# A start-up reordering in a joint-softmax classifier kernel: two products move to GpSimd, two sums are split, idle matmuls are cut, first products and tail waits are reordered

## The reference

```
variables = [softmax(p) for p in split(logits, 4)]      # v0, v1, v2, v3: 512 x 16 each
flat = outer(v0, v1, v2, v3).reshape(512, 65536)
num_y_joint = einsum('bj,by->yj', flat, y_true)          # 100 x 65536
num_joint = sum(flat, axis=0)                            # 65536
prob_y_joint = clip(max(num_y_joint, 1e-6) / max(num_joint, 1e-6), 0, 1)
probs = einsum('yj,bj->by', prob_y_joint, flat)          # 512 x 100
```

## Time and profile before

| | |
|---|---|
| time, median of 3 runs | 534.98 us (534.86 to 535.18) |
| time of the profiled execution | 535.27 us |
| its span in the profile | 533.2 us |
| PE busy | 529.1 us, 99% |
| DVE busy | 296.3 us, 56% |
| ACT busy | 41.7 us, 8% |
| POOL busy | 23.1 us, 4% |

### The profile page before, as it was taken

The page is one execution under the profiler, slowest core; times in us unless marked ns, Lnnn a source line. Parts: engine busy times, 40 slices in busy tenths (PEclk is TensorE's granted clock), DMA queues, the critical chain, the costliest instruction groups (busy, mean ns, idle before and its releaser), DMA issues.

```text
span 533.2 us, 8646 instructions
## 1 busy us (share of the span) xinstructions
PE 529.1 (99%) x3115; PEld 305.0 (57%) x3115; DVE 296.3 (56%) x763; ACT 41.7 (8%) x96; POOL 23.1 (4%) x21
## 2 busy tenths in 40 slices
PE   9999999999999999999999999999999999999997
PEld 5555555555555555555555555555555555555555
DVE  7986766764585444444467544444446544444446
ACT  7950000000200000000020000000001000000000
POOL 0000000000140000000032000000004000000000
PEclk9999999999999999999999999999999999999999
DMA  2944434220000000000000000000000000000000
GB/s 45 159 80 79 59 62 79 46 54 1 1 0 1 1 0 0 0 0 0 1 0 1 1 0 0 0 0 0 0 0 1 1 0 0 0 0 0 1 1 17
DMA packets 34771, 9.21 MB, mean 17 GB/s; under 512 B 34496, under 2 KB 34752, under 8 KB 34752
## 3 DMA queue, kind: packets, MB, share of 16 engines
q1 hardware_dynamic: 34752, 8.93, 9.5%
HBM read 0.34 MB, written 0.20 MB: 1 GB/s over the span
## 4 chain that ended last, share of the span: by engine, by line
PE 99%; DVE 0%; issue 0%; POOL 0%; DVEq 0%; POOLq 0%
PE joined L454 16%; PE joined L456 16%; PE joined L455 16%; PE numbers L446 16%; PE numbers L447 16%; PE numbers L448 16%; PE numbers L470 1%; PE numbers L476 1%; PE numbers L479 1%; PE numbers L473 1%; DVE acc L413 0%; PE numbers L576 0%; PE numbers L573 0%; PE numbers L572 0%; PE joined L567 0%; PE joined L564 0%
## 5 line engine op out<-in xcount | busy, mean ns | idle before, releaser
L456 PE MATMUL joined<-r_hi,pt_lo 128*128 128x400 f16 x504 | 167.6, 332 | 0.0
L455 PE MATMUL joined<-r_lo,pt_hi 128*128 128x400 f16 x504 | 167.6, 332 | 0.0
L454 PE MATMUL joined<-r_hi,pt_hi 128*128 128x400 f16 x504 | 167.5, 332 | 0.0
L446 PE MATMUL numbers<-q_hi,p_hi 128*128 128x404 f16 x492 | 164.8, 335 | 0.0
L448 PE MATMUL numbers<-q_hi,p_lo 128*128 128x404 f16 x492 | 164.0, 333 | 0.0
L447 PE MATMUL numbers<-q_lo,p_hi 128*128 128x404 f16 x492 | 163.9, 333 | 0.0
L333 DVE TENSOR_SCALAR den<-numbers 128x4 f32<-128x4 f32 x128 | 20.7, 162 | 211.4 <-PE numbers L448 211.3
L345 DVE SCALAR_TENSOR_TENSOR r_lo<-ratio,r_hi 128x400 f16<-128x400 f32 x128 | 78.3, 612 | 4.4
L338 DVE SCALAR_TENSOR_TENSOR ratio<-numbers,inv 128x400 f32<-128x400 f32 x128 | 73.5, 574 | 4.4
L455 PEld LDWEIGHTS joined<-r_lo,pt_hi 128*128 (+1 forms) x504 | 49.2, 98 | 36.3
L454 PEld LDWEIGHTS joined<-r_hi,pt_hi 128*128 (+1 forms) x504 | 49.1, 97 | 36.3
(11 more groups left out here) (53 smaller groups left out, 87.1 us busy)
## 6 DMA issues: line engine op xcount, KB each, us to landing
pt_hi<-p_hi SPq DMA_TRANSPOSE x16, 3.1
pt_lo<-p_lo SPq DMA_TRANSPOSE x16, 3.2
labels<-in_r_y_true_dram SPq DMA_DIRECT2D x1, 200.0 KB, 3.0
out_dram<-acc SPq DMA_DIRECT2D x1, 150.0 KB, 1.8
x<-in_r_logits_dram SPq DMA_DIRECT2D x1, 128.0 KB, 2.1
out_dram<-acc SPq DMA_DIRECT2D x1, 50.0 KB, 1.5
```

The lines of the kernel that those rows point to most:

```text
L446: pe.matmul(out, p_at(p_hi, tile, k), q_at(q_hi, g, k), start=(k == 0), stop=False)
L454: pe.matmul(out, p_at(pt_hi, tile, k), r_hi[:, slot, :], start=first, stop=False)
L455: pe.matmul(out, p_at(pt_hi, tile, k), r_lo[:, slot, :], start=False, stop=False)
L456: last = pe.matmul(out, p_at(pt_lo, tile, k), r_hi[:, slot, :], start=False, stop=final)
```

## The change

GpSimd no longer zeroes `idle` (VectorE does) and, behind the wait for the first exponentials, makes p23 of chunks 0 and 1 in two instructions with a semaphore of their own (`p23_first`). VectorE drops `make_p23(0, 2)` and sums v2, v3 and then v0, v1 in two reductions. ScalarE waits for `p23_first`. TensorE has 24 idle matmuls (14, 5, 3, 2) in place of 31, and the second batch waits for the exponentials and not for p23. Some of the first 48 products change place, none is added or dropped. In the tail the waits for `added` and for `half_ready` change order in the source.

```diff
-        IDLE_START, IDLE_EXPS, IDLE_V0, IDLE_Q = 18, 6, 4, 3
+        IDLE_START, IDLE_EXPS, IDLE_V0, IDLE_Q = 14, 5, 3, 2
...
-            pool.memset(idle[:, :], 0.0).then_inc(idle_set, 1)
             pool.memset(labels[:, :, CLASSES:CW], 1.0).then_inc(ones_set, 1)
             pool.memset(acc[:, :, :], 0.0).then_inc(acc_set, 1)
+            pool.wait_ge(exps, 1)
+            for k in range(2):
+                pool.tensor_tensor(p23[:, k, :].rearrange("p (c d) -> p c d", d=S),
+                                   ek[:, k, 2, :].unsqueeze(2).broadcast_to([LANES, S, S]),
+                                   ek[:, k, 3, :].unsqueeze(1).broadcast_to([LANES, S, S]),
+                                   ALU.mult).then_inc(p23_first, 1)
...
-            act.wait_ge(p23_made, 1)
+            act.wait_ge(p23_first, 1)
             first_p_hi(0, 0)
+            act.wait_ge(p23_first, 2)
             first_p_hi(0, 1)
...
+            dve.memset(idle[:, :], 0.0).then_inc(idle_set, 1)
             dve.wait_ge(logits_in, 16)
...
             dve.wait_ge(exps, 1)
-            make_p23(0, 2)
+            dve.tensor_reduce(sums[:, :, 2:4], ek[:, :, 2:4, :], AX.X, ALU.add).then_inc(reduced, 1)
             dve.wait_ge(exps, 2)
-            dve.tensor_reduce(stat[:, 1, :], x[:, :, :], AX.X, ALU.add).then_inc(reduced, 1)
-            dve.wait_ge(reduced, 1)
+            dve.tensor_reduce(sums[:, :, 0:2], ek[:, :, 0:2, :], AX.X, ALU.add).then_inc(reduced, 1)
+            dve.wait_ge(reduced, 2)
             dve.tensor_reduce(whole[:, :], sums, AX.X, ALU.mult).then_inc(reduced, 1)
...
             for a in range(AG):
+                dve.wait_ge(added, KC * AG + a)
                 if a % HA == 0:
                     dve.wait_ge(half_ready, a // HA + 1)
-                dve.wait_ge(added, KC * AG + a)
                 add(KC - 1, a, numbers[a // HA], a % HA)
...
             pe.wait_ge(idle_set, 1)
             idle_turns(IDLE_START)
-            pe.wait_ge(p23_made, 1)
+            pe.wait_ge(exps, 1)
             idle_turns(IDLE_EXPS)
```

More of the change, by code:

```diff
@@ L115, in joint_classifier @@
         v0n_made = sem("v0n_made")
+        p23_first = sem("p23_first")
         p23_made = sem("p23_made")
@@ L247, in _ @@
             first_p_hi(1, 1)
-            act.wait_ge(p23_made, 2)
+            act.wait_ge(p23_made, 1)
             first_p_hi(0, 2)
@@ L348, in _ @@
             dve.wait_ge(exps, 1)
-            make_p23(0, 2)
+            dve.tensor_reduce(sums[:, :, 2:4], ek[:, :, 2:4, :], AX.X, ALU.add).then_inc(reduced, 1)
             dve.wait_ge(exps, 2)
-            dve.tensor_reduce(stat[:, 1, :], x[:, :, :], AX.X, ALU.add).then_inc(reduced, 1)
-            dve.wait_ge(reduced, 1)
+            dve.tensor_reduce(sums[:, :, 0:2], ek[:, :, 0:2, :], AX.X, ALU.add).then_inc(reduced, 1)
+            dve.wait_ge(reduced, 2)
             dve.tensor_reduce(whole[:, :], sums, AX.X, ALU.mult).then_inc(reduced, 1)
-            dve.wait_ge(reduced, 2)
+            dve.wait_ge(reduced, 3)
             dve.reciprocal(whole[:, :], whole[:, :]).then_inc(whole_made, 1)
@@ L505, in _ @@
             lo_hi(1, 1)
-            pe.wait_ge(q_ready, 1)
-            hi_lo(0, 0)
-            hi_lo(1, 0)
             pe.wait_ge(p_hi_made, 4)
@@ L511, in _ @@
             hi_hi(3, 1)
-            hi_lo(2, 0)
-            hi_lo(3, 0)
+            pe.wait_ge(q_ready, 1)
+            for tile in range(4):
+                hi_lo(tile, 0)
+            pe.wait_ge(q_ready, 2)
+            hi_lo(0, 1)
+            hi_lo(1, 1)
             pe.wait_ge(p_hi_made, 5)
@@ L517, in _ @@
             hi_hi(1, 2)
-            pe.wait_ge(q_ready, 2)
-            for tile in range(4):
-                hi_lo(tile, 1)
+            hi_lo(2, 1)
+            hi_lo(3, 1)
+            pe.wait_ge(p_ready, 3)
+            lo_hi(2, 0)
+            lo_hi(3, 0)
             pe.wait_ge(p_hi_made, 6)
@@ L524, in _ @@
             hi_hi(1, 3)
-            pe.wait_ge(p_ready, 3)
-            lo_hi(2, 0)
-            lo_hi(3, 0)
             pe.wait_ge(p_ready, 4)
```

## The result

The changed kernel takes **534.12 us** (median of 22 runs, 533.93 to 534.45); the kernel before, run beside it, 534.88 us (22 runs, 534.70 to 535.18). The ratio is 0.9985, 95% interval 0.9980 to 0.9991: 0.76 us or 0.14% faster. The ranges of the two do not touch, so the gain is real, and it is under the 0.2% that the prediction counted as a change.

A forecast was written before the change was run, and what follows sets the result against it. TensorE, busy 529.1 of 533.2 us, was taken as the bound. Start 0.60 plus tail 0.15 gave 0.75 us, or 0.30 with an early clock rise; 0.5 was taken, so 534.5 us, range 534.0 to 535.3.

The forecast's parts named there:

- What bounds the kernel: Whole kernel: TensorE is busy 529.1 of 533.2 us, so only its real start, starving after it and the tail count.
- The clock: TensorE's start: the clock rises from 1.2 to 2.4 GHz at about 6.9 us; starting earlier than that gains half.
- The case that I had as the second one: Start-up: the clock rises before the idle matmuls end; gain 0.15 at the start plus 0.15 in the tail, 0.30 us.
- The rival with a later rise: Gaps between idle matmuls delay the clock's rise; 2 to 3.5 us of delay would give 535.3 to 536.0; chance 0.05.
- Step 1, GpSimd: Start-up: each p23 product of 256 elements takes GpSimd 0.71 us, the two done at 4.67 and 5.38.
- Step 2, the sums: VectorE's start: half sums take 0.28 us each; without anything else qf would start 0.45 us earlier.
- Step 3, the two together: VectorE's qf, reading SBUF beside GpSimd, ends at 5.87 against 6.05; VectorE's list moves 0.17 us, not 0.45.
- Step 4, idle matmuls: TensorE's start: 24 idle matmuls no longer reach the first product; effective start 6.70, 0.60 us earlier.
- Step 5, the feed: First products: waits for q_lo of chunk 1 and p_lo of chunk 3 ask for 6.67 and 6.63, met by 6.70.
- Step 6, the tail: Last additions: swapping the two waits saves some 0.07 us at two additions, 0.15 us; bounds 0 and 0.15.
- The rival with the code library: GpSimd's start: a library load by DMA delays it 3.0 us and costs 3 us, 538 to 540; chance 0.10.

The follow-up runs named there:

- e1_tail: The kernel before with only the two tail waits swapped; 534.75 us, 0.19 us faster than before, with an interval that holds no change.
- e8: The changed kernel with 14 idle matmuls and none behind the later waits; 535.51 us, 0.52 us slower than the kernel before.
- e12: The changed kernel with GpSimd's second product held until VectorE's first qf is made; 535.27 us, 0.33 us slower than the kernel before.
- e6: The changed kernel with a third p23 product, chunk 2, on GpSimd; 534.33 us, 0.66 us faster than the kernel before.
- e4: The changed kernel with p23 of chunks 0 and 1 back on VectorE; 534.63 us, 0.31 us faster than the kernel before.
- e2: The kernel before with 24 idle matmuls in place of 31 and nothing else; 534.89 us, 0.05 us faster than before.
- e3: The changed kernel with its idle matmuls back at 31; 534.32 us, 0.62 us faster than the kernel before.
- e7: The kernel before with p23 on GpSimd, sums split, zeroing on VectorE and the second idle batch behind `exps`; 534.58 us, 0.41 us faster.
- e9: The changed kernel run again, unaltered; 534.16 us, 0.78 us faster than the kernel before.

## Why the prediction was right or wrong

The range (534.0 to 535.3) held 534.12 near its low end, and within 0.2% was right: what was to shorten the start and the tail did so. The value, 534.5, had 0.5 us of gain where 0.76 was measured. That it is no further off is in part luck. The 0.75 us of its sum were meant for an execution whose clock rises at 6.9 us; for an early rise it gave 0.30, and there the traces show 0.75, 9.25 - 8.64 = 0.61 at the start and 0.14 in the tail. The old kernel's bound was put at 6.83 us and its 35th product shows 12.87 - 5.81 = 7.06 in e1_tail; the new one's was put at 6.67, and it shows 12.20 - 5.81 = 6.39 (0.06 us of the difference is that e1_tail's exponentials began that much later). By the steps:

- **What bounds the kernel.** Right that only the start and the end count. But that TensorE "works off idle matmuls that are too many by 0.6 us" was a property of one execution, with the clock's rise at 6.9 us. In e1_tail the same 31 ended in time for a first product at 6.92, and the operands set the 35th.
- **The clock.** The pricing (a start at the low clock is worth half) is borne out by e8, 0.34 against 0.17 us a product. The case that I had as the second one is the usual one: in twelve of the thirteen other traces the clock rises between 4.0 and 6.7 us; in e8 it rises at 9.3. The rival with a later rise did not come true for the changed kernel, whose rests before the first product are 0.3 us at most; e8, after 2.18 us of rest, shows its mechanism.
- **Step 1, GpSimd.** This is the term that was mis-sized: 0.71 us a product by the rows for 64 and 400 elements; two took 1.20, so it is 0.60, near the lower figure that the rows for 64 and 1600 gave, 0.61.
- **Step 2, the sums.** Right: 0.28 to 0.29 us each.
- **Step 3, the two together.** Mechanism right: qf ended 0.43 us behind GpSimd, as r_lo did in the earlier trace rows, without the further 0.06 us that I had added; e12 and e6 show the exclusion itself. With 1.20 in place of 1.42 us for the two products it ends at 5.58 and not at 5.87. So "0.17 us, not 0.45" failed: the supply moved by 0.46 us, 0.42 without the earlier exponentials, and nearly the whole of it was won. The Trainium skill (SBUF — State Buffer, "Who interferes with whom") has two SBUF inputs beside a GpSimd read exclude each other, and these runs agree in that; but qf ended 0.43 us behind GpSimd and not its whole 0.64. What the Trainium skill says there of a tensor_reduce, that it never waits, is now seen too: the half sums took 0.29 and 0.28 us beside GpSimd's products, and 0.28 each in e4, where GpSimd makes none.
- **Step 4, idle matmuls.** The 0.60 us were put down to them and to the supply together. Cut alone they are worth 0.05 us (e2); with the earlier supply, the longer spans among the runs of e3 and e7 speak for a start that 31 of them hold in some executions.
- **Step 5, the feed.** The two waits that I named as the tightest are the ones: q_lo of chunk 1 held the 17th product for 0.09 us, and p_lo was there just in time for the 35th. The old order's bound was set too low, by looking at q_lo of chunk 0 and not at q_hi of chunk 2; the order is worth 0.17 us.
- **Step 6, the tail.** Right: 0.13 to 0.14 us for 0.15.
- **The rival with the code library** fell: GpSimd began 0.05 us behind VectorE, which waits for the same exponentials. The Trainium skill's figure of about 6 us (GPSIMD Engine Reference, "Instruction dispatch") is for a freshly loaded kernel, and no such delay shows here.

The new account, from traces in which the clock rose at 6.2 us or earlier: GpSimd and the sums 0.43, the order 0.17, the tail 0.14, together **0.74 us** for 0.76 measured; the cut of the idle matmuls nothing there. How the executions are mixed, the spans of the timed runs tell. Of the kernel before's 101 runs beside the experiments, 20 have spans of 533.1 to 533.3 us, as its profile has, and 81 of 532.8 to 533.0; the changed kernel's 33 runs have 532.0 to 532.4. So about a fifth of the old kernel's executions pay for a late clock, some 0.3 us each (9.52 - 9.25 = 0.27 in the measure), and the changed kernel's runs have no such group. That the clock's rise is what parts the runs in this way is inferred: one execution of each kernel was profiled.

## What to carry to other kernels

A profile is one execution: when an engine's start hangs on something that varies, such as the clock's rise, find the second limit behind it (here operands, 12.87 and 12.88 with 31 and 24 idle matmuls) before the first is priced. Work moved to GpSimd beside VectorE costs VectorE the overlap where VectorE reads two operands from SBUF; here it was free beside reductions, and in one row beside work on a PSUM bank, so put it there, and move only as much as fits. When two waits stand before one instruction, let the instruction itself carry the one that comes last. And test how far filler work can be cut: with 24 idle matmuls no run of the changed kernel stood apart (in e12, whose first product comes 1.1 us later, four of twelve did), with 14 the median lost 1.3 to 1.4 us.

## What the runs showed of the hardware that was not expected

The clock's rise moved freely between executions of nearly the same start-up: 31 idle matmuls took 6.38, 6.00 and 5.17 us in three kernels that all begin them between 1.04 and 1.08, and their starts draw together, from 0.213 us apart to 0.109, at 6.9 us in the kernel before, 5.1 in the changed one and 4.0 in the same kernel again (e9). GpSimd's first arithmetic of the program cost no more than its second: 0.62 us alone in e12, 1.20 for two. GpSimd can be the one that waits: 0.79 us beside VectorE's p_lo in e12. And two waits in front of one VectorE instruction cost 0.06 to 0.07 us when the late one is not its own.
